# Edge banks of a graph layer anchored at a first node read from the list, on one Trainium2 core

## The reference

```
def layer(x, src, dst, W_self, W_neigh, b):           # x: 1250 x 512, 20000 edges, dst sorted
    msg = segment_sum(x[src], dst, 1250)
    deg = segment_sum(ones, dst, 1250)
    h = x @ W_self + (msg / max(deg, 1)) @ W_neigh + b
    h = where(h >= 0, h, 0.01 * h)
    return h / max(sqrt(sum(h * h, axis=1)), 1e-12)

def ffn(x, w_gate, w_up, w_down):                     # 512 -> 1408 -> 512
    # each weight row in groups of 128: scale = mean(abs) + 1e-5,
    # weight = clip(round(w / scale), -1, 1) * scale
    return (silu(x @ gate.T) * (x @ up.T)) @ down.T

x = x + layer(layernorm(x), src, dst, ...)
return x + ffn(layernorm(x), ...)
```

## Time and profile before

| | us |
|---|---|
| median of three runs | 368.21 |
| the profiled execution's own time | 368.42 |
| its span, first to last instruction | 366.4 |
| busy: PE / PEld | 338.5 / 260.0 |
| busy: DVE / ACT / POOL | 307.5 / 236.0 / 162.0 |
| granted TensorE clock, mean | 0.995 of full speed |

### The profile page before, as it was taken

One profiled execution on the slowest core, in us unless ns is written; L12 is line 12 of the kernel. 1 busy time (PEld: TensorE's weight loads), 2 busy tenths in 40 slices (PEclk: granted clock), 3 DMA queues, 4 the chain that ended last, 5 costly groups with the idle time before them and its releaser, 6 DMA issues.

```text
span 366.4 us, 5873 instructions
## 1 busy us (share of the span) xinstructions
PE 338.5 (92%) x1741; PEld 260.0 (71%) x1741; DVE 307.5 (84%) x745; ACT 236.0 (64%) x638; POOL 162.0 (44%) x186
## 2 busy tenths in 40 slices
PE   2978999999999999999766999999999999999992
PEld 1435555555655668777655988889899898889991
DVE  2599999699788339999788798999999998999994
ACT  2255978678667225775456777677676678776670
POOL 3001101100000292100003366888788886799992
PEclk9999999999999999999989999999999999999999
DMA  7942223222122001200000000000000000000215
GB/s 225 306 140 58 69 76 88 58 69 78 56 76 74 13 1 30 79 22 1 2 0 2 0 1 2 0 3 1 0 2 0 3 2 2 0 0 3 68 47 168
DMA packets 9411, 16.69 MB, mean 46 GB/s; under 512 B 1062, under 2 KB 1886, under 8 KB 9378
## 3 DMA queue, kind: packets, MB, share of 16 engines
q1 hardware_dynamic: 9300, 16.21, 15.2%
q10 hardware_dynamic: 78, 0.08, 0.1%
HBM read 13.73 MB, written 2.56 MB: 44 GB/s over the span
## 4 chain that ended last, share of the span: by engine, by line
PE 72%; DVE 18%; ACT 4%; issue 2%; POOL 1%; DVEq 0%; ACTq 0%; POOLq 0%
PE bank L1200 39%; PE bank L1089 16%; PE bank L1050 6%; PE bank L1129 5%; DVE hot_dst L904 2%; DVE tq_d L841 2%; PE bank L1041 2%; PE bank L465 2%; DVE bn L946 2%; DVE x_sb L943 1%; DVE bn L827 1%; DVE z L925 1%; PE bank L1112 1%; DVE tq_gu L841 1%; DVE z L931 1%
## 5 line engine op out<-in xcount | busy, mean ns | idle before, releaser
L1200 PE MATMUL bank<-x_hi,t_gu 128*128 128x378 f32 (+1 forms) x264 | 96.2, 364 | 3.6 <-DVE x_lo L960 2.8
L1200 PE MATMUL bank<-x_lo,t_gu 128*128 128x378 f32 (+1 forms) x264 | 94.8, 359 | 0.0
L1089 PE MATMUL bank<-w_sb,xnT 128*125 128x512 f32 x160 | 86.0, 624 | 1.5 <-ACT z L670 0.8
L999 DVE SCALAR_TENSOR_TENSOR g_acc<-bank,nscale,g_acc 128x378 f32<-128x378 f32 (+1 forms) x99 | 64.3, 650 | 11.9 <-PE bank L1200 11.3
L562 POOL TENSOR_SCALAR thr<-absum 128x4 f32<-128x4 f32 (+1 forms) x34 | 12.7, 373 | 123.3 <-ACT mag_early L640 99.8
L999 DVE SCALAR_TENSOR_TENSOR u_acc<-bank,nscale,u_acc 128x378 f32<-128x378 f32 (+1 forms) x99 | 64.0, 647 | 0.6 <-PE bank L1200 0.6
L583 POOL TENSOR_TENSOR acc<-acc,d_one 128x378 f32<-128x378 f32 (+1 forms) x58 | 61.0, 1054 | 0.1
L593 POOL TENSOR_TENSOR hh<-sg,u_acc 128x378 f32<-128x378 f32 (+1 forms) x32 | 35.1, 1097 | 57.6 <-ACT sg L770 57.5
L1050 PEld LDWEIGHTS bank<-hot_dst,hot_src 128*125 128x125 bf16 x281 | 32.4, 137 | 39.6 <-issue 21.6
L1200 PEld LDWEIGHTS bank<-x_hi,t_gu 128*128 128x128 f32 x264 | 50.5, 191 | 8.1 <-DVE x_lo L960 3.5
L904 DVE TENSOR_SCALAR hot_dst<-iota,key 128x400 bf16<-128x400 uint16 x157 | 44.7, 320 | 11.8 <-PE bank L1050 11.2
(11 more groups left out here) (107 smaller groups left out, 537.2 us busy)
## 6 DMA issues: line engine op xcount, KB each, us to landing
raw<-in_L_ffn_w_gate SPq DMA_DIRECT2D x11, 256.0 KB, 2.7
raw<-in_L_ffn_w_up SPq DMA_DIRECT2D x11, 256.0 KB, 2.6
out_x<-x_sb SPq DMA_DIRECT2D x10, 224.0 KB
raw<-in_L_ffn_w_down SPq DMA_DIRECT2D x8, 256.0 KB, 2.7
x_sb<-in_x SPq DMA_DIRECT2D x1, 1344.0 KB
w_sb<-in_L_gnn_W_neigh SPq DMA_DIRECT2D x1, 1024.0 KB, 6.3
w_sb<-in_L_gnn_W_self SPq DMA_DIRECT2D x1, 1024.0 KB, 6.7
raw<-in_L_ffn_w_down SPq DMA_DIRECT2D x4, 192.0 KB, 2.4
```

Source lines behind the costliest of these rows:

```text
L999: nc.vector.scalar_tensor_tensor(out=to, in0=bank_of(u, what)[:, 0:w], scalar=nscale[:, j:j + 1], in1=to, op0=ALU.mult, op1=ALU.add).then_ ...
L1089: last = nc.tensor.matmul(to[0:TP, :], xnT[:, t, k * TP:(k + 1) * TP], w_sb[:, k, half * D:(half + 1) * D], start=k == 0, stop=k == KD - 1)
L1200: last = nc.tensor.matmul(to, w, parts[h], start=h == 0, stop=h == 1)
```

## The change

Blocks are no longer 40 fixed destination nodes. Blocks 1 to 30 are five chunks each (640 edges; block 0 has two chunks, block 31 five), and such a block is anchored at the destination node of its first edge, which is read from the list (`base_f`, clamped to 0..1200; the last block starts at node 1200). A bank is 10 source tiles by 50 nodes from there. Each of the five chunks has a fixed window within the bank (WINS: 14, 18, 20, 22 and 26 nodes wide, 20 on the mean), so every chunk is one matmul, and `hot_dst` is as wide as the window: 140 to 260 columns. Two more small fp32 matmuls at slot 1 bring the first node of each chunk to all partitions.

Neighbouring blocks share one node. ACT copies columns 1 to 49 of a bank to `a_t` at an offset held in a register, and DVE adds column 0 (`join`, 10 values per partition, for the last block 420) onto what the block before left there. ACT and DVE read the 32 anchors into registers with one load each. PE may start block k once block k - 3 is joined, and the first neighbour sum once all blocks are. HOT is 7.

The test of the windows moves from before the slots to slot 20 (13 instructions, `check_windows`) and its flag to slot 27; PE reads it at slot 31. The bias is added to z by DVE as it takes z out of PSUM at slot 8t + 1, in place of ACT's copy and POOL's addition. LOADS1 falls from 25 to 22 loads: 11 ternary blocks leave the slots (88 remain) and go to the second stage, whose 44 blocks are spread by DOWN_PACE. POOL makes five more number rows and 35 small fills at the start.

```
-WIN = 40
+WIN = 50
...
+    SC = 5
+    NB = 1 + NC // SC
+    LASTB = N - WIN
+    WINS = [(0, 14), (4, 22), (11, 31), (18, 40), (24, 50)]
+    WINS_0 = [(0, 14), (4, 30)]
+    WINS_N = [(8, 31), (17, 38), (26, 45), (35, 50), (45, 50)]
...
-    HOT = 5
+    HOT = 7
...
+    DEG_BLOCKS = [11, 20]
+    CHECK, FLAG = 20, 27
...
+        first_chunk = [0] + [2 + SC * (k - 1) for k in range(1, NB)]
+        last_chunk = [c - 1 for c in first_chunk[1:]] + [NC - 1]
+
         def window(c):
 
-            k, off = divmod(STEP * c - LEAD, WIN)
-            parts = [(k, off, 0, WIN - off), (k + 1, 0, WIN - off, off)]
-            return [p for p in parts if 0 <= p[0] < NB and p[3]]
+            k = max(k for k in range(NB) if first_chunk[k] <= c)
+            return k, *(WINS_0 if k == 0 else WINS_N if k == NB - 1 else WINS)[c - first_chunk[k]]
+
+        def chunk_used(c):
+
+            k = window(c)[0]
+            return (block_done, k + 1) if c == last_chunk[k] else (hot_used, c + 1 - k)
...
-        LOADS1 = 2 * NF + 3
+        LOADS1 = 2 * NF
...
+        DOWN_PACE = [0, 3, 5, 7, 8, 9, 10, 11, 12, 12, 12]
...
+            for j, (lo, hi) in enumerate(WINS):
+                nc.gpsimd.iota(iota_w[j][:], pattern=[[WIN, NT], [1, hi - lo]], base=lo, channel_multiplier=0,
+                               allow_small_or_imprecise_dtypes=True).then_inc(rows_set, 1)
+            nc.gpsimd.memset(a_t[:, :, LASTB:N].bitcast(F32), 0.0).then_inc(zeroed, 1)
+            nc.gpsimd.memset(base_f[:, 0:1], 0.0).then_inc(zeroed, 1)
+            nc.gpsimd.memset(base_f[:, NB - 1:NB], float(LASTB)).then_inc(zeroed, 1)
...
-            pool.wait_ge(bias_in, 16)
-            pool.wait_ge(block_out, NB)
-            for t in range(NT):
-                pool.wait_ge(z_out, t + 1)
-                nc.gpsimd.tensor_tensor(z[:, t, :], z[:, t, :], bias_b[0:TP, :], ALU.add).then_inc(z_done, 1)
...
+                if slot == FIRST + 1:
+                    act.wait_ge(prep, 9)
+                    _, bases = nc.values_load_multi_w_load_instructions(
...
-                if i == 2 and 1 <= t <= NT:
-                    act.wait_ge(z_ready, t)
-                    nc.scalar.activation(z[:, t - 1, :], bank[6][0:TP, :], ACT.Copy).then_inc(z_out, 1)
...
+                        if k == NB - 1:
+                            continue
                         act.wait_ge(block_done, k + 1)
-                        n = min(WIN, N - k * WIN)
-                        nc.scalar.activation(
-                            a_t[:, :, k * WIN:k * WIN + n],
-                            bank[k % 3][0:TP, 0:NT * WIN].rearrange("p (s d) -> p s d", d=WIN)[:, :, 0:n],
-                            ACT.Copy).then_inc(block_out, 1)
+                        if k == 0:
+                            act.wait_ge(zeroed, 3)
+                            to, cols = a_t[:, :, 0:WINS_0[-1][1]], slice(0, WINS_0[-1][1])
+                        else:
+                            act.wait_ge(block_out, k)
+                            to, cols = a_t[:, :, 1:N][:, :, bass.ds(bases[k], WIN - 1)], slice(1, WIN)
+                        nc.scalar.activation(to, bank[k % 3][0:TP, 0:NT * WIN].rearrange("p (s d) -> p s d", d=WIN)[:, :, cols],
+                                             ACT.Copy).then_inc(block_out, 1)
...
+            dve.wait_ge(zeroed, 3)
+            link(nc.vector.tensor_scalar(base_f[:, 1:NB - 1], firsts[:, first_chunk[1]:first_chunk[NB - 1]:SC], float(LASTB), 0.0,
+                                         ALU.min, ALU.max))
+            nc.vector.tensor_copy(rel[:, 0:first_chunk[1]], dsts[:, 0:first_chunk[1]]).then_inc(prep, 1)
+            steps[0] += 1
+            link(nc.vector.tensor_tensor(rel[:, first_chunk[1]:NC].rearrange("p (k j) -> p k j", j=SC),
+                                         dsts[:, first_chunk[1]:NC].rearrange("p (k j) -> p k j", j=SC),
+                                         base_f[:, 1:NB, None].to_broadcast([P, NB - 1, SC]), ALU.subtract))
+            nc.vector.tensor_copy(base_i[:], base_f[:]).then_inc(prep, 1)
+            steps[0] += 1
+            link(nc.vector.scalar_tensor_tensor(out=key[:, 0:NC], in0=src_hi[:, 0:NC], scalar=float(WIN), in1=rel[:, 0:NC],
+                                                op0=ALU.mult, op1=ALU.add))
+            link(nc.vector.tensor_copy(dst_f[:], dsts))
+            assert steps[0] == 11
...
-            dve.wait_ge(edges_T, 2)
-            link(nc.vector.tensor_scalar(flag[:], bank[5][:, 2 * NCP:2 * NCP + 1], float(E), None, ALU.is_lt))
-            any_outside = dve.value_load(flag[0:1, 0:1])
+            dve.wait_ge(rows_set, SC)
+
+            def check_windows():
...
+                dve.wait_ge(rows_set, SC + 2 * (len(WINS_0) + len(WINS_N) + SC) + 5)
+                link(nc.vector.tensor_tensor(win_lo[:, 0:NC], rel[:, 0:NC], win_lo[:, 0:NC], ALU.subtract))
...
+                link(nc.vector.tensor_scalar(gap_ok[:], gap[:], 0.0, None, ALU.is_ge))
+                nc.vector.scalar_tensor_tensor(out=gap[:], in0=least[:], scalar=0.0, in1=gap_ok[:], op0=ALU.is_ge, op1=ALU.mult,
+                                               accum_out=inside[:, 1:2]).then_inc(checked, 1)
...
+            def join(k):
+
+                dve.wait_ge(block_out, min(k + 1, NB - 1))
+                if k == NB - 1:
+                    dve.wait_ge(block_done, NB)
+                cols = slice(0, 1) if k < NB - 1 else slice(WINS_N[0][0], WIN)
+                to = a_t[:, :, bass.ds(bases[k], 1)] if k < NB - 1 else a_t[:, :, LASTB + WINS_N[0][0]:N]
+                nc.vector.tensor_tensor(to, bank[k % 3][0:TP, 0:NT * WIN].rearrange("p (s d) -> p s d", d=WIN)[:, :, cols],
+                                        to.bitcast(F32), ALU.add).then_inc(joined, 1)
...
+                if i == 1 and 1 <= t <= NT:
+                    dve.wait_ge(z_ready, t)
+                    if t == 1:
+                        dve.wait_ge(bias_in, 16)
+                    nc.vector.tensor_tensor(z[:, t - 1, :], bank[6][0:TP, :], bias_b[0:TP, :], ALU.add).then_inc(z_out, 1)
...
+                        k, lo, hi = window(c)
+                        numbers, to = iota_w[c - first_chunk[k]][:] if 0 < k < NB - 1 else None, hot_dst[:, c % HOT, 0:NT * (hi - lo)]
+                        if numbers is None:
+                            numbers = iota[:, 0:NT * WIN].rearrange("p (s d) -> p s d", d=WIN)[:, :, lo:hi]
+                            to = to.rearrange("p (s d) -> p s d", d=hi - lo)
+                        nc.vector.tensor_scalar(to, numbers, key[:, c:c + 1], None, ALU.is_equal).then_inc(hot_made, 1)
+                if slot == FIRST + 2:
+                    dve.wait_ge(prep, 9)
+                    _, bases = nc.values_load_multi_w_load_instructions(
...
+                for k in blocks_ending(slot - 2):
+                    if k:
+                        join(k)
+                if slot == CHECK:
+                    check_windows()
+                if slot == FLAG:
...
-                dve.wait_ge(z_done, t + 1)
+                dve.wait_ge(z_out, t + 1)
...
-                parts = window(c)
-                for k, d0, w0, n in parts:
-                    if c == first_chunk[k] and k >= 3:
-                        pe.wait_ge(block_out, k - 2)
-                    last = nc.tensor.matmul(
-                        bank[k % 3][0:TP, 0:NT * WIN].rearrange("p (s d) -> p s d", d=WIN)[:, :, d0:d0 + n],
-                        hot_src[:, c // SB % SBS, c % SB, 0:TP],
-                        hot_dst[:, c % HOT, :].rearrange("p (s d) -> p s d", d=WIN)[:, :, w0:w0 + n],
-                        start=c == first_chunk[k], stop=c == last_chunk[k], skip_group_check=True)
-                    if c == last_chunk[k]:
-                        last.then_inc(block_done, 1)
-                    elif (k, d0, w0, n) == parts[-1]:
-                        last.then_inc(hot_used, 1)
+                k, lo, hi = window(c)
+                if c == first_chunk[k] and k >= 3:
+                    if k == 3:
+                        pe.wait_ge(block_out, 1)
+                    else:
+                        pe.wait_ge(joined, k - 3)
+                nc.tensor.matmul(bank[k % 3][0:TP, 0:NT * WIN].rearrange("p (s d) -> p s d", d=WIN)[:, :, lo:hi],
+                                 hot_src[:, c // SB % SBS, c % SB, 0:TP],
+                                 hot_dst[:, c % HOT, 0:NT * (hi - lo)].rearrange("p (s d) -> p s d", d=hi - lo),
+                                 start=c == first_chunk[k], stop=c == last_chunk[k],
+                                 skip_group_check=True).then_inc(block_done if c == last_chunk[k] else hot_used, 1)
...
+                if slot == CHECK + 3:
+                    pe.wait_ge(checked, 1)
+                    for h in range(2):
+                        last = nc.tensor.matmul(bank[7][:, 0:1], ones[:], inside[:, h:h + 1], start=h == 0, stop=h == 1)
+                    last.then_inc(edges_T, 1)
+                if slot == FLAG + 4:
```

(5 more changed lines are left out.)

119 lines of the change are left out of this document (80 added, 39 removed).

## The result

The changed kernel takes **366.7 us** in the median (20 runs, 366.44 to 368.72), the kernel before 369.0 us beside it (20 runs, 368.12 to 370.23). The ratio is 0.995, with a 95% interval of 0.994 to 0.997: by the ratio 1.8 us faster (the medians differ by 2.3), where 5.6 were forecast. The profiled execution shown here took 368.50 us, span 366.6.

The account below looks back on a forecast made before the run. PE set the pace before, DVE would bound the changed first stage. Second stage 7.2 us earlier less 1.6 lost gives 5.6; 368.42 becomes 362.8, less 0.2 for the median, 362.6 us, range 356 to 371.

Parts of the forecast that it names:

- PE's part: First stage, PE: 31,330 fewer one-hot columns at 0.54 us per 1200 save 14.1 us; two more fp32 matmuls cost about 0.5.
- Prices of DVE's instructions: First stage, DVE: one-hot step 0.18 us, z 0.60, join 0.15, test 3.7, anchors' load 1.0; 99.3 us of work.
- So DVE reaches that point at 15.6 + 93.9 + 1 of waits = 110.5: First stage, slot 74: DVE's start, work and waits were added to give when its last ternary blocks are done.
- the start: Start of the first stage: DVE begins at 15.6 us instead of 17.8, with 0.5 added for later first-node transposes.
- DVE becomes the bound: First stage: DVE, at 99.3 us of work against PE's 90, sets the time.
- Second stage: Second stage: ternary blocks moved there delay steps 2 and 3; 1.6 us lost, bounds 0.3 and 2.9.
- The third: Rival, three engines in lock-step: small waits return 2 to 4 us, second stage takes 2.9; 366.5 us, chance 0.15.
- The first: Rival on DVE's one-hots: time goes with width, step 0.13 us; 354.4 us, chance 0.09.
- the fourth: Rival on DVE's one-hots: they get no faster, step 0.23 us; 370.6 us, chance 0.06.
- The second: Rival on DVE's joins: each costs about 0.55 us instead of 0.15, 12 us in all; 374.6 us, chance 0.12.
- The fifth: Rival: an edge outside its window sends the kernel down the general path, 4000 one-hot pairs, milliseconds; chance 0.01.
- 7.2 earlier: End of the first stage: the second stage starts at 117.8 us instead of 125.0.

Follow-up runs that it names:

- the combination: Changed kernel with window test spread over slots 40 to 52, POOL's fills later, slot 10's statistics spread, first-node transposes signalled apart: 361.9, 360.8 and 361.0 us.
- the one with the late fills: Changed kernel with POOL's new fills and number rows started only after DVE's first normalization: 367.1 us, ratio 0.991 to the kernel before.

## Why the prediction was right and wrong

- **Direction, and PE's part: right.** 0.09 us per 200 columns gives 7.6 us for the 85 chunks of slots 28 to 68; measured 8.5, and 7.8 without the test.
- **Prices of DVE's instructions: right.** The test takes 3.7 us (45.04 to 48.72). The one-hot's step is 0.18 us: two of them, from 78.18, end where the join starts, at 78.54. z steps by 0.60, and the anchors' load ahead of the first z shows 0.63 us for the 1.0 that was taken. The join holds DVE for 0.08 us and not for 0.15. (157 x 0.052 is 8.2 and not 8.0, which changes nothing here.)

```profile
78.18 0.45 DVE L1004 TENSOR_SCALAR hot_dst<-iota_w,key 128x260 bf16<-128x260 uint16 x2
78.54 0.17 DVE L964 TENSOR_TENSOR a_t<-bank,a_t 125x10 f32 x1
78.62 0.35 DVE L895 SCALAR_TENSOR_TENSOR tq_gu<-mag_early,thr,raw 128x128 bf16<-128x128 f32 x1
...
85.03 0.68 DVE L983 TENSOR_TENSOR z<-bank,bias_b 125x512 f32<-125x512 f32 x1
85.63 0.45 DVE L1004 TENSOR_SCALAR hot_dst<-iota_w,key 128x200 bf16<-128x200 uint16 x2
```

- **Where it failed.** The step "So DVE reaches that point at 15.6 + 93.9 + 1 of waits = 110.5". Its inputs were sums over the whole stage, and the larger of the two engines' sums was taken as the time. In the changed kernel's profile DVE was done with the stage's last ternary block, just ahead of slot 74, at 115.35 us, 4.85 later than the step says. Three things were wrong in it. *First*, the 1 us of waits: the waits of DVE from 20 to 125 us come to 13 us, 11.8 of them in the rows shown above, and 9.7 of them lie ahead of the 115.35. With 16.85 to 124.0 as the stage that leaves some 94 us of DVE work, less than the 99.3 forecast: the work was priced too high, the waits far too low. *Second*, the start: the later first-node transposes were put at 0.5 us and took 1.29, and `xn` beside POOL's fills, put at nothing, took 1.1 more. DVE began at 16.85 and not 15.6, then stood 2.34 us for ACT's root, which was queued behind ACT's copy of `xnT`, which waited for PE's transposes of slot 4; so it reached the statistics of slot 10 at 25.83, after 23.62 before the change. The prediction had followed only DVE's chain there. *Third*, the test counted at its duration on DVE. At slot 20 neither PE nor ACT has anything to go on with, so the whole of it reached PE as a wait, and with the clock behind it PE paid 5.5 to 6.1 us for 3.7.
- **"DVE becomes the bound"** was half of the truth. In slots 28 to 68 of the changed kernel PE is full and DVE has 3 us in 40 to spare:

```profile
60.00:100.00 40.00, 40.00 (x176) 21.18 (x175) 36.96 (x146) 31.80 (x116) 3.34 (x11) 1.00 0.26 73
```

  In part that is because the halt at slot 20 had already made PE late: without the test the same slots take 50.77 us instead of 50.03. And the room is smaller than it looks, since the eleven blocks cost 2.3 us behind slot 28 even there. In the combination both engines are full at once, as its variants with z on ACT and with the eleven blocks show. What one-off work DVE has early in the stage is not made good later, because the later slots have little slack for it. A stage's time is the sum of what each stretch takes at its slowest engine, and that is more than the slowest engine's sum.
- **Second stage: right in kind.** 1.6 us lost were forecast (0.3 to 2.9), 0.9 to 1.1 measured. In the profiles step 2 starts 18.94 us after the stage's first matmul (142.44 less 123.50) instead of 17.77, close to the 1.1 us forecast for it. The transposes, now at 152.81, come 1.2 us later in the stage than in the earlier trace rows.
- **The rivals.** The third, with 366.5 us, gave the time, and in DVE's waits also part of the mechanism; it named neither the test nor the clock, which were the larger part, so its number was partly luck. The first and the fourth fell with the one-hot's step of 0.18 us. The second fell too: ahead of the joins DVE stood 3.0 us in all, 2.7 of them in five waits for ACT, where 12 us were its price. The fifth, with milliseconds, did not occur.
- **The sum again.** Forecast: 7.2 earlier, 1.6 lost. Mean of the profiles: the first neighbour matmul at 122.6 instead of 125.3, 2.7 earlier; 0.9 lost in the second stage, and 0.4 in the third, whose instructions are the same and where in these five profiles the granted clock is below 1.00 in some stretches from 180 to 204 us; no run takes that 0.4 apart. Of the 4.5 us missing in the first stage, 2 are the test's excess over 3.7 us; the rest goes to the start and to DVE's waits up to slot 28, which no run divides between them.

## What to carry to other kernels

When a change puts a one-off block of work on an engine that feeds another, ask first how far ahead that engine is at that place: the same 13 instructions cost 6 us where there was no lead, 3 us in one piece behind a lead, and 1 us spread over 13 slots. Cut a stage at milestones that both programs have and forecast each piece by its own slowest engine; two engines that are nearly equal over the whole stage will each be the slower one somewhere, and the sum misses that. And profile the kernel before twice before building on a microsecond of it.

## What was not expected of the hardware

- **The clock behind a wait.** In all six profiles in which PE waited 3.05 to 3.21 us for the test at slot 20, the granted clock then fell to the 1.2 GHz level, for some 7 us in five of them and about half of that in the sixth, the one with the ternary blocks back. Behind the wait of 3.3 to 3.6 us at slot 10 it fell in four of eight profiles, and behind one of 1.5 us in two of eight. Behind eleven waits of 1.65 to 2.63 us, the one at the test with z on ACT among them, it stayed at 1.00. So a wait of 3.2 us cost PE up to nearly twice its length (5.5 to 6.1 us), and a wait of the same length elsewhere did so in some executions only. The Trainium skill ("TensorE: Matmul & The Clock Gate", Part 1) describes a gate that puts the array back to its slow clock after idleness, on a count of its own that doesn't start with the kernel and so makes the moment vary from run to run; the four of eight agree with that. Why the short waits of 1.5 us sufficed twice is open.
- **The start.** From 9 us on, projection records of PE step by 0.85 us instead of 0.43 while the granted clock reads 1.00, with PE busy all the while. The last full step of 0.85 us ends at 14.0 us in the first profile of the kernel before, at 15.7 in its second, and between 14.4 and 18.9 in the eighteen others. Why is open.
- **POOL beside DVE.** While POOL wrote constants, DVE's normalization of 125x512 took 1.69 us against 0.55 with POOL held back, as these rows of the changed kernel and of the one with the late fills show. The Trainium skill ("SBUF — State Buffer", "SBUF: two separate sides") says that VectorE and GpSimd share a pair of ports, which one instruction holds exclusively to its end; on VectorE's side it names instructions in a mode that uses both of its port pairs, or with two inputs in SBUF against a GpSimd instruction that reads SBUF. The two rows fit such a block, but the mode of this instruction stands in no row, and which of POOL's instructions held it was not tried.

```profile
5.67 1.69 DVE L875 TENSOR_SCALAR xn<-x_sb,mv,rs 125x512 f32<-125x512 f32 x1
```

```profile
5.68 0.55 DVE L876 TENSOR_SCALAR xn<-x_sb,mv,rs 125x512 f32<-125x512 f32 x1
```
